# Low halves of the next batch's rotated query and key rows: from VectorE to GpSimd

## The chip, the core and the metric

One core of a Trainium2 chip runs the whole program. The metric is device time in microseconds (us). The engines are TensorE (PE: matrix products, with its weight loads as PEld), VectorE (DVE), ScalarE (ACT), GpSimd (POOL) and SyncE (SP, which here only issues DMAs). Each engine works off its own list of instructions in order, and waits on semaphores that the others raise.

## The reference

A post-norm decoder layer on x of 4 batches x 512 rows x 512 values: causal self-attention with 16 heads of 32 and keys and values from a latent of 128, then attention over 512 context rows that keeps the 54 highest scores, then a mixture of 8 experts, with a layer norm after each. The change touches the first block alone:

```
q = (x @ Wq).reshape(B, S, HEADS, HEAD_DIM).transpose(0, 2, 1, 3)
c_kv = x @ Wkv_down
k = (c_kv @ Wk_up).reshape(...)
v = (c_kv @ Wv_up).reshape(...)
q_rope = _apply_rope(q_rope, cos, sin)   # 24 of each head's 32 values; the same for k
scores = jnp.einsum('bhqd,bhkd->bhqk', qf, kf) * scale
weights = jax.nn.softmax(jnp.where(causal, -jnp.inf, scores), axis=-1)
out = jnp.einsum('bhqk,bhkd->bhqd', weights, v)
x = _layernorm(x + out)
```

## The kernel before

A product is made from 16-bit halves: each operand is split into a high half (rounded to f16) and a low half (what the rounding left), and three products high x high, high x low, low x high are summed. Queries and keys carry this in their transposed rows: `cat` holds, for each of the 8 row blocks of a batch (4 blocks of 128 rows, query and key of each), the high half twice and the low half once.

The first block works a batch at a time, and while it finishes the heads of batch b it already prepares batch b+1. Five lists, one for each computing engine (`A_PE`, `A_ACT`, `A_DVE`, `A_POOL`; SP's stands in code), set the order of the units by hand. A unit is a name and a number. The ones in this text:

- `row.i` (PE, line 952, then ACT, line 1240): the i-th block of queries (even i) or keys (odd i) is computed, and copied to the buffer `rows`, which has four places, i mod 4.
- `rope.i` (POOL, line 777): four instructions rotate that block in place: two multiplications (`turn_a`, `turn_b`, line 785), a subtraction (788) and an addition (790).
- `rhi.i` (ACT, line 1258): the high half goes into `cat`. `rlo.i` (DVE, lines 1545 to 1548): the low half is the difference of `rows` and the high half.
- `q0.i`, `k0.i`, `q1.i`, `k1.i` (PE, line 968): transposes of `cat`, copied out by DVE (q, line 1555) and ACT (k). They wait for `cat_lo`, which each `rlo` raises.
- `bq.i` and `max.i`: head i's scores with queries on the partitions, and their row maxima (DVE, four reductions, line 1566). `mT.i`: the maxima of four heads are transposed (PE) and copied into `qcT` (DVE, line 1576).
- `bk.i`, `exp.i`, `hi.i`, `lo.i`, `pv.i`: scores with keys on the partitions, their exponential (ACT), its high half (ACT) and low half (12 of the 16 heads, six by DVE and six by POOL, the latter at line 795), and the product with the values.
- `v.i`, `comb.i`, `res.i`: values of the next batch; heads put together; batch b-1's residual sum with its moments.
- `ln.0` (ACT a square root, DVE lines 1602 to 1609): batch b-1's layer norm. On DVE it is five small instructions (lines 1524 to 1528), and then four that scale 128x512 values each (line 1609).

The loop over b runs three times (b = 0, 1, 2); the last batch's heads follow without a next part. The first of the three has no `res` and no `ln`. The start-up lists, which prepare batch 0, are others (`A_START_DVE` and so on). A PSUM bank is shared by units as `A_BANK` says: `row.7` and `mT.2` both use bank 7, so PE's `row.7` waits until DVE has copied `mT.2` out. `row.6` waits so for `v.2`.

Of the kernel before, what the change touches and what calls it, by code (L numbers as in the profile page):

```python
# [30 lines left out]
TT = S // P  # L31
# [33 lines left out]
A_NEXT = ("xT", "c", "row", "rope", "rhi", "rlo", "v", "q0", "k0", "bqn", "maxn", "mTn")  # L65
# [15 lines left out]
def steps(text):  # L81

    return [(k, int(i)) for k, i in (word.split(".") for word in text.split())]
# [14 lines left out]
""")  # L98
A_DVE = steps("""
    xT.0 xT.1 q1.0 max.5 xT.2 xT.3 q1.1 res.0 lo.0 q1.2 max.6 res.1 c.0 q1.3  # L100
    max.7 res.2 mT.1 rlo.0 max.8 rlo.1 v.0 max.9 rlo.2 res.3 max.10 v.1 lo.4 rlo.3 max.11 v.2
    ln.0 max.12 rlo.4 mT.2 max.13 lo.6 q0.0 rlo.5 max.14 q0.1 comb.0 q0.2 max.15
    lo.8 rlo.6 rlo.7 q0.3 mT.3 maxn.0 comb.1 lo.12 maxn.1 comb.2 maxn.2
    lo.14 maxn.3 v.3 mTn.0 maxn.4 comb.3
""")
A_POOL = steps("""
    rope.0 lo.1 rope.1 lo.2 rope.2 rope.3 rope.4 rope.5 lo.5 rope.6 rope.7 lo.9
    lo.10 lo.13 
""")

# [21 lines left out]
def next_part(seq, kinds):  # L132
    return [u for u in seq if u[0] in kinds]
# [139 lines left out]
def decoder(nc, a):  # L273
    ctx = ExitStack()

    def sem(name):
        return ctx.enter_context(nc.semaphore(name))

    def sb(stack, name, shape, dt=F32):
        return stack.enter_context(nc.sbuf_tensor(name, shape, dt))  # L280

    with ctx:
# [31 lines left out]
        rows = sb(sa, "rows", [P, 4, H, HD])  # L314
# [3 lines left out]
        cat = sb(sa, "cat", [P, 2 * TT, H, 3, HD], F16)  # L318
# [99 lines left out]
        cat_hi = sem("cat_hi")  # L418
        cat_lo = sem("cat_lo")
# [80 lines left out]
        def a_upto(b, u):  # L500

            return b * A_PER[A_KIND.get(u[0], u[0])] + (u[1] + 1 + FREE)
# [231 lines left out]
        def _(pool):  # L734
# [40 lines left out]
            def heads(seq, b, nxt):  # L775
                for k, i in seq:
                    if k == "rope":

                        n, t = nxt * (2 * TT) + i, i // 2
                        pool.wait_ge(a_drained["row"], a_upto(nxt, ("row", i)))  # L780
                        pool.wait_ge(roped, n * 4 + FREE)
                        pair = rows[:, i % 4, :, NOPE:HD].rearrange("p h (i two) -> p h i two", two=2)
                        for j, dst in ((0, turn_a), (1, turn_b)):
                            cs = cossin[:, j, t].unsqueeze(1).to_broadcast([P, H, ROPE // 2, 2])
                            nc.gpsimd.tensor_tensor(dst[:, :, :, :], pair, cs, ALU.mult).then_inc(roped, 1)  # L785
                        pool.wait_ge(roped, n * 4 + (2 + FREE))
                        half = NOPE + ROPE // 2
                        nc.gpsimd.tensor_tensor(rows[:, i % 4, :, NOPE:half], turn_a[:, :, :, 0], turn_a[:, :, :, 1],
                                                ALU.subtract).then_inc(roped, 1)
                        nc.gpsimd.tensor_tensor(rows[:, i % 4, :, half:HD], turn_b[:, :, :, 1], turn_b[:, :, :, 0],  # L790
                                                ALU.add).then_inc(roped, 1)
                    elif k == "lo":

                        pool.wait_ge(p_hi, b * len(HALVED) + (HALVED.index(i) + 1))
                        nc.gpsimd.tensor_tensor(plo[:, i % 2, :], pf[:, i % 2, :], phi[:, i % 2, :], ALU.subtract).then_inc(p_lo_pool, 1)  # L795

            heads(next_part(A_POOL, A_NEXT), None, 0)
            pool.wait_ge(roped, 2 * TT * 4 + FREE)
            with pool.Fori(0, B - 1) as b:
                heads(A_POOL, b, b + 1)  # L800
            heads(own_part(A_POOL, A_NEXT), B - 1, None)


# [1177 lines left out]
```

## Time and profile before

| | |
|---|---|
| median of 3 runs | 1636.16 us (1635.18 to 1636.54) |
| the profiled execution | 1635.91 us, its span 1634.1 us |
| PE busy | 1471.2 us, 90% of the span |
| DVE, ACT, POOL busy | 1186.5, 900.4, 767.7 us |
| the three passes of the loop | 99 to 375 us of the span, roughly |

Times in the trace are us from the span's start. An instruction's duration in the trace runs from where its engine took it up, so it holds the time in which the engine stood on it. What an engine waited for before an instruction stands in brackets. The chain of waits is followed back from the last instruction: at each step to what released it. Its piece "issue" is time in which the profile shows no cause.

### The profile page before, as it was taken

The page shows a single profiled execution, that of the slowest core. Times are in us where ns is not written, and L with a number is a line of the kernel's source. Part 1 is how long each engine was busy: PE and PEld are TensorE (multiplying, and loading weights), DVE is VectorE, ACT ScalarE, POOL GpSimd, SP SyncE. Part 2 cuts the span into 40 slices and gives each one's busy share as a digit, 9 for nine tenths or more (in the row PEclk, how much of TensorE's full clock was granted, in tenths as well). Part 3 has the DMA queues.
Part 4 walks back from the last instruction along what each step waited for, and adds up shares of the span by engine and source line. Part 5 has one row for each costly group of instructions (what it writes and reads, how often), then busy time and mean ns, then how long its engine had stood idle before and what let it go on. Part 6 is the DMA issues. An engine that isn't in the chain of part 4 may idle for free.

```text
span 1634.1 us, 27867 instructions
## 1 busy us (share of the span) xinstructions
PE 1471.2 (90%) x10404; PEld 902.3 (55%) x10404; DVE 1186.5 (73%) x2030; ACT 900.4 (55%) x1452; POOL 767.7 (47%) x693
## 2 busy tenths in 40 slices
PE   6898888988788898587999999999999999999984
PEld 3466666566544454243665666566656665666554
DVE  4767787968459999967776667666766676667657
ACT  4367575766544553555465556555655565556542
POOL 5355362712212314888474456445644564456422
PEclk9799988988599999788999999999999999999997
DMA  9500010002011110210010001000110011000002
GB/s 288 213 27 2 29 53 29 27 28 104 27 52 52 52 53 1 65 66 13 27 40 26 27 26 36 31 27 27 35 32 27 26 29 37 27 27 28 12 1 103
DMA packets 68173, 74.72 MB, mean 46 GB/s; under 512 B 9021, under 2 KB 46525, under 8 KB 67017
## 3 DMA queue, kind: packets, MB, share of 16 engines
q1 hardware_dynamic: 67464, 68.73, 13.0%
q10 hardware_dynamic: 576, 4.19, 0.7%
q8 instruction: 88, 1.44, 0.4%
q14 instruction: 45, 0.36, 0.1%
HBM read 49.66 MB, written 10.49 MB: 37 GB/s over the span
## 4 chain that ended last, share of the span: by engine, by line
PE 65%; DVE 13%; issue 8%; POOL 6%; ACT 4%; DVEq 0%; ACTq 0%; POOLq 0%
PE banks L1177 48%; PE banks L920 6%; PE banks L1029 2%; PE banks L1013 2%; DVE nmf L1566 2%; PE banks L974 2%; PE banks L991 1%; POOL xsum L824 1%; POOL xsum L821 1%; ACT pf L1271 1%; DVE top L1698 1%; DVE wk L1694 1%; PE banks L1015 1%; DVE attf L1705 1%; POOL xc L829 1%
## 5 line engine op out<-in xcount | busy, mean ns | idle before, releaser
L1177 PE MATMUL banks<-xc,w 128*128 128x512 f16 x2688 | 588.7, 381 | 15.8 <-ACT banks L1220 15.8
L1177 PEld LDWEIGHTS banks<-xc,w 128*128 128x128 f16 x2688 | 263.7, 98 | 335.4 <-ACT banks L1220 21.2
L1177 PE MATMUL banks<-wd,mid 128*128 128x256 f16 x2688 | 296.5, 273 | 4.7 <-ACT banks L1220 2.8
L1177 PEld LDWEIGHTS banks<-wd,mid 128*128 128x128 f16 x2688 | 262.8, 98 | 39.3 <-ACT banks L1220 3.1
L897 POOL TENSOR_TENSOR mid<-m,mid 128x512 f16<-128x512 f32 x64 | 75.0, 1172 | 315.0 <-ACT mid L1220 314.9
L1220 ACT ACTIVATE banks<-banks 128x512 f32<-128x512 f32 x192 | 108.3, 578 | 186.5 <-PE banks L1177 186.5
L897 POOL TENSOR_TENSOR mid<-msum,mid 128x512 f16<-128x512 f32 x128 | 185.8, 1470 | 1.3 <-ACT mid L1220 1.3
L1511 DVE SCALAR_TENSOR_TENSOR w<-stage,w 128x512 f16<-128x512 f32 (+1 forms) x56 | 62.2, 1150 | 104.4 <-ACT w L1220 104.4
L1220 ACT ACTIVATE mid<-msum 128x512 f16<-128x512 f32 x128 | 81.1, 634 | 85.4 <-DVE msum L1881 29.2
L795 POOL TENSOR_TENSOR plo<-pf,phi 128x1280 f16<-128x1280 f32 x24 | 63.8, 2665 | 117.1 <-ACT phi L1220 116.9
L1566 DVE TENSOR_REDUCE nmf<-banks 128x1 f32<-128x512 f32 (+3 forms) x256 | 107.2, 481 | 10.2 <-PE banks L993 9.8
L1271 ACT ACTIVATE pf<-banks 128x1280 f32<-128x1280 f32 x64 | 79.1, 1236 | 38.9 <-PE banks L1015 21.9
L785 POOL TENSOR_TENSOR turn_a<-rows,cossin 128x384 f32<-128x384 f32 x32 | 35.9, 1123 | 121.1 <-ACT rows L1220 120.3
L1220 ACT ACTIVATE xc<-banks 128x512 f32<-128x512 f32 (+1 forms) x112 | 62.8, 598 | 49.5 <-PE banks L1124 28.5
L897 POOL TENSOR_TENSOR mid<-xc,mid 128x512 f16<-128x512 f32 x32 | 52.4, 1638 | 69.2 <-ACT mid L1220 69.2
L1013 PE MATMUL banks<-qcT,kcT 100*128 100x512 f16 (+3 forms) x256 | 71.4, 355 | 13.2 <-ACT pf L1271 11.8
L1511 DVE SCALAR_TENSOR_TENSOR wd<-stage,wd 128x512 f16<-128x512 f32 (+1 forms) x32 | 29.4, 960 | 65.9 <-ACT wd L1220 65.9
L1843 DVE TENSOR_TENSOR xc<-banks,xc 128x512 f32<-128x512 f32 x96 | 63.1, 683 | 17.3 <-ACT banks L1220 17.3
L1843 DVE TENSOR_TENSOR s<-banks,s 128x512 f32<-128x512 f32 x96 | 64.2, 684 | 14.1 <-PE banks L1177 14.0
L991 PE MATMUL banks<-kcT,qcT 96*128 96x512 f16 (+3 forms) x256 | 67.6, 338 | 5.2 <-DVE nmf L1566 3.9
L1220 ACT ACTIVATE s<-banks 128x512 f32<-128x512 f32 x96 | 56.3, 602 | 25.9 <-PE banks L1177 25.8
L1220 ACT ACTIVATE phi<-pf 128x1280 f16<-128x1280 f32 x48 | 60.9, 1269 | 1.2 <-PE banks L1034 1.2
(253 smaller groups left out, 2967.0 us busy)
## 6 DMA issues: line engine op xcount, KB each, us to landing
stage<-w_fold SPq DMA_DIRECT2D x24, 256.0 KB, 2.9
stage<-in_Wg SPq DMA_DIRECT2D x24, 256.0 KB, 3.2
stage<-in_Wu SPq DMA_DIRECT2D x24, 256.0 KB, 3.1
stage<-in_Wd SPq DMA_DIRECT2D x24, 256.0 KB, 2.8
vcat<-vnext SPq DMA_DIRECT2D x8, 528.0 KB, 3.3
x_in<-in_x SPq DMA_DIRECT2D x4, 1024.0 KB, 6.5
x_res<-in_x SPq DMA_DIRECT2D x4, 1024.0 KB, 5.8
c_raw<-in_ctx SPq DMA_DIRECT2D x4, 1024.0 KB, 5.5
```

The lines of the kernel that those rows point to most:

```text
L785: nc.gpsimd.tensor_tensor(dst[:, :, :, :], pair, cs, ALU.mult).then_inc(roped, 1)
L795: nc.gpsimd.tensor_tensor(plo[:, i % 2, :], pf[:, i % 2, :], phi[:, i % 2, :], ALU.subtract).then_inc(p_lo_pool, 1)
L897: nc.gpsimd.tensor_tensor(mid16[:, v % 3, 1, blk], mid_value(name), mid16[:, v % 3, 0, blk], ALU.subtract)\
L920: mm = nc.tensor.matmul(out, l(x, i), r(y, i), start=(i == 0 and j == 0), stop=(i == n - 1 and j == 2))
L991: nc.tensor.matmul(score[:, o:o + w], qcT[0:K3, i, t * P:(t + 1) * P], kcT[0:K3, i, 0:w], start=True, stop=False)
L1013: nc.tensor.matmul(st_ps[:, o:o + w], kcT[0:K3 + G, i, t * P:(t + 1) * P], qcT[0:K3 + G, i, t * P:S], start=True, stop=False)
L1177: mm = nc.tensor.matmul(out, l(x, i), r(y, i), start=start and i == 0 and j == 0, stop=stop and i == k - 1 and j == 2, skip_group_check=True)
L1220: return nc.scalar.activation(out, in_, ACT.Copy, scale=scale)
L1271: nc.scalar.activation(pf[:, i % 2, :], st_ps[:, 0:TRI], ACT.Exp, scale=1.0 / (SQ * SQ * math.sqrt(HD))).then_inc(exp_done, 1)
L1511: return stt(out=out, in0=src, scalar=scale, in1=hi, op0=ALU.mult, op1=ALU.subtract)
L1566: nc.vector.tensor_reduce(nmf[:, t, i % G:i % G + 1], max_bank(b, i)[:, o:o + w], AX, ALU.max, negate=True)\
L1843: tt_(saved, banks[:, k, :], saved, ALU.add).then_inc(c_sum, 1)
```

## The change

Eight units `rlo.0` to `rlo.7` leave DVE's list and go into POOL's. `rlo.i` stands there one rotation behind `rope.i`: `rlo.0` behind `rope.1`, and so on, with `rlo.7` last of them. `rlo.0` stands ahead of `lo.2`, `rlo.4` ahead of `lo.5`, and `rlo.7` ahead of `lo.9`. POOL gets the code for it, the same subtraction with the same wait for `rhi` (semaphore `cat_hi`), raising `cat_lo`. The start-up's `rlo` stay on DVE, so the call that prepares batch 0 now takes `rope` alone. No DMA, buffer or bank changes.

```
@@ -98,13 +98,13 @@
 A_DVE = steps("""
...
-    max.7 res.2 mT.1 rlo.0 max.8 rlo.1 v.0 max.9 rlo.2 res.3 max.10 v.1 lo.4 rlo.3 max.11 v.2
-    ln.0 max.12 rlo.4 mT.2 max.13 lo.6 q0.0 rlo.5 max.14 q0.1 comb.0 q0.2 max.15
-    lo.8 rlo.6 rlo.7 q0.3 mT.3 maxn.0 comb.1 lo.12 maxn.1 comb.2 maxn.2
+    max.7 res.2 mT.1 max.8 v.0 max.9 res.3 max.10 v.1 lo.4 max.11 v.2
+    ln.0 max.12 mT.2 max.13 lo.6 q0.0 max.14 q0.1 comb.0 q0.2 max.15
+    lo.8 q0.3 mT.3 maxn.0 comb.1 lo.12 maxn.1 comb.2 maxn.2
...
 A_POOL = steps("""
-    rope.0 lo.1 rope.1 lo.2 rope.2 rope.3 rope.4 rope.5 lo.5 rope.6 rope.7 lo.9
+    rope.0 lo.1 rope.1 rlo.0 lo.2 rope.2 rlo.1 rope.3 rlo.2 rope.4 rlo.3 rope.5 rlo.4 lo.5 rope.6 rlo.5 rope.7 rlo.6 rlo.7 lo.9
     lo.10 lo.13 
@@ -789,12 +789,16 @@
+                    elif k == "rlo":
+                        pool.wait_ge(cat_hi, nxt * (2 * TT) + (i + 1))
+                        dst = cat[:, i, :, 2] if i % 2 == 0 else cat[:, i, :, 1]
+                        nc.gpsimd.tensor_tensor(dst, rows[:, i % 4], cat[:, i, :, 0], ALU.subtract).then_inc(cat_lo, 1)
...
-            heads(next_part(A_POOL, A_NEXT), None, 0)
+            heads(next_part(A_POOL, ("rope",)), None, 0)
```

POOL's list inside the loop, before, from `rope.5` to `lo.5` (line 785 are the two multiplications of a rotation, 788 and 790 its end, 795 the low half of a head's exponentials):

```order
L780 REGISTER_ALU
L781 ISA
L785 TENSOR_TENSOR turn_a<-rows,cossin 128x384
L785 TENSOR_TENSOR turn_b<-rows,cossin 128x384
L786 REGISTER_ALU
L788 TENSOR_TENSOR rows<-turn_a 128x16x12
L790 TENSOR_TENSOR rows<-turn_b 128x16x12
L794 REGISTER_ALU
L795 TENSOR_TENSOR plo<-pf,phi 128x1280
```

The same place in the changed kernel, from `rlo.3` on; lines behind the new code have moved by four, so `lo` is line 799 and line 795 is the new subtraction:

```order
L795 TENSOR_TENSOR cat<-rows,cat 128x16x32
L780 REGISTER_ALU
L781 ISA
L785 TENSOR_TENSOR turn_a<-rows,cossin 128x384
L785 TENSOR_TENSOR turn_b<-rows,cossin 128x384
L786 REGISTER_ALU
L788 TENSOR_TENSOR rows<-turn_a 128x16x12
L790 TENSOR_TENSOR rows<-turn_b 128x16x12
L795 TENSOR_TENSOR cat<-rows,cat 128x16x32
L798 REGISTER_ALU
L799 TENSOR_TENSOR plo<-pf,phi 128x1280
```

Two `rlo` now stand around this rotation, and the second of them ahead of `lo.5`.

DVE's list in the loop, before, from the end of `ln.0` over `max.12` and `rlo.4` (line 1548) to `mT.2` (line 1576):

```order
L1609 TENSOR_SCALAR resid<-resid,mv,rstd 128x512 x4
L1564 ISA
L1566 TENSOR_REDUCE nmf<-banks 128x1
L1564 REGISTER_ALU
L1566 TENSOR_REDUCE nmf<-banks 128x1 x2
L1564 REGISTER_ALU
L1566 TENSOR_REDUCE nmf<-banks 128x1
L1546 REGISTER_ALU
L1548 TENSOR_TENSOR cat<-rows,cat 128x16x32
L1574 REGISTER_ALU
L1576 COPY qcT<-banks 4x2048
```

The same place in the changed kernel:

```order
L1613 TENSOR_SCALAR resid<-resid,mv,rstd 128x512 x4
L1568 ISA
L1570 TENSOR_REDUCE nmf<-banks 128x1
L1568 REGISTER_ALU
L1570 TENSOR_REDUCE nmf<-banks 128x1 x2
L1568 REGISTER_ALU
L1570 TENSOR_REDUCE nmf<-banks 128x1
L1578 REGISTER_ALU
L1580 COPY qcT<-banks 4x2048
```

`mT.2` now follows `max.12` directly.

## Rows read from the trace of the kernel before

**Rows 1.** The page, part 1: busy time, share, instructions of each engine.
```profile
PE 1471.2 (90%) x10404; PEld 902.3 (55%) x10404; DVE 1186.5 (73%) x2030; ACT 900.4 (55%) x1452; POOL 767.7 (47%) x693
```

**Rows 2.** Busy time, second pass: length, PE, PEld, DVE, ACT, POOL, PE clock, DMA.
```profile
188.00:281.00 93.00, 82.95 (x943) 59.94 (x942) 72.84 (x133) 64.91 (x85) 43.37 (x38) 0.89 0.11 36
```

**Rows 3.** Chain of waits, second pass: start, us, what it ran through.
```profile
199.12 0.71 POOL plo L795
...
208.38 0.92 POOL rows L790
...
222.12 1.14 issue
...
224.54 1.46 PE banks L920 x3
```

**Rows 4.** PE in time order at `row.7`: start, us, instruction, wait before it.
```profile
224.54 1.03 PE L920 MATMUL banks<-wku,cT 128*128 128x512 f16 x2 [2.35 <-DVE qcT L1576]
```

**Rows 5.** Busy time by stretch behind that wait, second and third pass (columns as Rows 2).
```profile
224.00:228.00 4.00, 3.46 (x20) 2.13 (x21) 3.57 (x6) 0.98 (x2) 3.17 (x5) 0.57 0.00 0
...
317.00:323.00 6.00, 5.71 (x33) 3.88 (x34) 5.09 (x9) 2.78 (x3) 5.09 (x6) 0.50 0.00 0
```

**Rows 6.** Line 1548, all of it: duration ns min/median/max, first and last start.
```profile
L1548 DVE TENSOR_TENSOR cat<-rows,cat x32: 674/693/1580, 28.0 to 332.5; 128x512 f16<-128x512 f32 x32
```

**Rows 7.** Line 808, a POOL subtraction of the same size and types in another stage.
```profile
L808 POOL TENSOR_TENSOR kq<-copyf,kq x16: 1152/1156/1161, 453.8 to 633.5; 128x512 f16<-128x512 f32 x16
```

**Rows 8.** POOL in time order, second pass.
```profile
201.66 1.44 POOL L785 TENSOR_TENSOR turn_a<-rows,cossin 128x384 f32<-128x384 f32 x1
...
215.24 0.99 POOL L785 TENSOR_TENSOR turn_a<-rows,cossin 128x384 f32<-128x384 f32 x1 [2.87 <-ACT rows L1220]
...
217.72 0.50 POOL L790 TENSOR_TENSOR rows<-turn_b 128x192 f32<-128x192 f32 x1
219.79 2.88 POOL L795 TENSOR_TENSOR plo<-pf,phi 128x1280 f16<-128x1280 f32 x1 [1.57 <-ACT phi L1220]
```

**Rows 9.** DVE in time order, second pass, ahead of it ACT's `v.1`.
```profile
210.29 0.64 ACT L1220 ACTIVATE vnext<-banks 128x128 f32<-128x128 f32 x2
...
212.12 1.59 DVE L1580 TENSOR_TENSOR plo<-pf,phi 128x1280 f16<-128x1280 f32 x1
213.63 0.68 DVE L1548 TENSOR_TENSOR cat<-rows,cat 128x512 f16<-128x512 f32 x1
...
216.64 0.16 DVE L1524 RECIPROCAL rstd<-rstd 128x4 f32<-128x4 f32 x1
...
220.11 1.68 DVE L1566 TENSOR_REDUCE nmf<-banks 128x1 f32<-128x512 f32 x4
221.70 1.52 DVE L1548 TENSOR_TENSOR cat<-rows,cat 128x512 f16<-128x512 f32 x1
223.26 1.23 DVE L1576 COPY qcT<-banks 4x2048 f16<-4x2048 f16 x1
```

**Rows 10.** POOL, then ACT, in time order, first pass.
```profile
125.53 0.99 POOL L785 TENSOR_TENSOR turn_a<-rows,cossin 128x384 f32<-128x384 f32 x1 [2.07 <-ACT rows L1220]
...
134.14 1.75 POOL L790 TENSOR_TENSOR rows<-turn_b 128x192 f32<-128x192 f32 x1
...
135.92 1.06 ACT L1220 ACTIVATE cat<-rows 128x1024 f16<-128x1024 f32 x1 [0.44 <-POOL rows L790]
```

**Rows 11.** Line 1609, all of it: duration ns min/median/max.
```profile
L1609 DVE TENSOR_SCALAR resid<-resid,mv,rstd x16: 539/544/547, 218.3 to 450.5; - x8, 128x512 f32<-128x512 f32 x8
```

**Rows 12.** DVE and POOL, a layer norm in the next stage, twice: POOL idle, POOL busy.
```profile
524.70 1.91 DVE L1742 TENSOR_SCALAR x2row<-x2row,mv,rstd 128x512 f32<-128x512 f32 x4
...
639.48 1.04 DVE L1525 TENSOR_TENSOR nwt<-rstd 128x4 f32<-128x4 f32 x1
...
642.10 3.71 DVE L1742 TENSOR_SCALAR x2row<-x2row,mv,rstd 128x512 f32<-128x512 f32 x4
643.27 1.33 POOL L824 TENSOR_TENSOR xsum<-xsum 128x512 f32<-128x512 f32 x1
```

## The prediction

> **What bounds the kernel now.** I read the page's busy times first, then the busy time by stretch over the loop's passes, then the chain of waits inside one pass, then each engine's list in time order where that chain changes engines. PE is busy for 90% of the span [rows 1], but in the second pass it is idle for some 10 of 93 us and its clock averages 0.89 of full speed [rows 2]; what a pass can gain or lose lies there. From 199 us on, the chain of waits runs through POOL (`lo.2`, `rope.2`, `rope.3`), through ACT's `v.1`, then through DVE (`lo.4`, `rlo.3`, `max.11`, `ln.0`, `max.12`, `rlo.4`, `mT.2`), and only then back to PE's `row.7` [rows 3]. The two engines between which the work moves thus stand one behind the other on that chain, and the question is which gains more.
>
> At `row.7` PE has stood for 2.35 us because `mT.2`'s bank was not copied out [rows 4], and after that its granted clock is at half, 1.2 GHz: 0.57 over 4 us in the second pass, 0.50 over 6 us in the third [rows 5]. Behind `row.7` PE works nearly without a gap, so a shift there moves the pass's end. The third pass repeats the second 92.8 us later. The first has no `ln.0`.
>
> **What leaves DVE.** Eight subtractions a pass. Alone one takes 0.69 us, but up to 1.58 [rows 6]: `rlo.0` stood behind POOL's `lo.2`, and POOL's next multiplication then stood behind it, 1.44 us instead of 0.99 [rows 8]. `rlo.4` took 1.52, right in front of `mT.2` [rows 9]. Were nothing else to change, `mT.2` would be copied out 1.5 us earlier. The `rlo` behind `mT.2` end no wait that PE feels, so I count them at nothing; DVE's idle time covers them.
>
> **What POOL gets.** Eight subtractions of 512 values. The trace has no such instruction on POOL for `cat`; the same size and types in another stage take 1.16 us, 1.15 to 1.16 in all 16 [rows 7]. The strided output might cost more; the multiplications, strided too, take 0.99 for 384 values [rows 8], which by count of values would be 1.32. I take 1.16, with 1.32 as the upper end; nothing in the trace is cheaper. Five of the eight stand ahead of `lo.5`. POOL now has waits to fill: 2.87 us for `row.5` and 1.57 for `hi.5` in the second pass [rows 8], 2.07 in the first [rows 10].
>
> **The second pass, POOL.** A rotation takes 2.98 us undisturbed (215.24 to 218.22) [rows 8]. From `lo.2`'s place at 199.1 [rows 3]: `rlo.0` to 200.2, `lo.2` (2.6) to 202.8, `rope.2` to 205.8, `rlo.1` to 207.5 (0.6 of that behind DVE's `res.3`, which now comes there), `rope.3` to 210.4. Now `rope.3` ends at 209.3 [rows 3], so it is 1.1 late. Then `rlo.2` to 211.6 and `rope.4`, with 1.4 us in which DVE's `lo.4` holds it, to 215.8; `rlo.3` to 216.9; `rope.5` would end at 219.8 alone, now 218.2. POOL has no wait left.
>
> **The second pass, DVE.** ACT does `rhi.3` before `v.1`, and `rhi.3` waits for `rope.3`. `v.1` ends on ACT at 210.9 now [rows 9], so 1.2 later, at about 212.1, then; DVE's own half of `v.1` follows it, and `lo.4` is issued at 212.7 rather than 212.12 [rows 9], stands behind a multiplication of `rope.4` until 213.5 and ends at 214.9. From there to `ln.0` takes 2.3 us (213.63 + 0.68 to 216.64) [rows 9]: `ln.0` starts at 217.2, against 216.64. All that DVE saved up to there has gone into waiting for ACT's `v.1`.
>
> Now comes the step that decides. `ln.0` takes 3.5 us today (216.64 to 220.11) [rows 9] since POOL is idle from 218.2 to 219.8 [rows 8]; the four scaling instructions never took over 0.55 [rows 11]. In the changed kernel POOL is busy throughout. What that does shows a stage later, where DVE does the same layer norm twice: with POOL idle its four scaling instructions take 1.91 us, and 3.71 beside POOL's subtractions of 1.3 us, one of which gets in between the first two; a small instruction ahead of them takes 1.04 [rows 12], where the one at 216.64 takes 0.16 [rows 9]. So the engines take turns: whoever waits goes next. POOL's turn in `ln.0` would hold the rest of `rope.5` (219.8 - 217.2 = 2.6), `rlo.4` (1.16), `lo.5` (2.6, ready because `hi.5` ends at 219.8 or a little later) and the next multiplication (1.0): 7.4 us, and DVE's own four 1.8. `ln.0` ends at 217.2 + 9.2 = 226.4, `max.12` (1.6) at 228.0, `mT.2` (1.23) at 229.2. Now `mT.2` ends at 224.5. The pass gets 4.7 us longer, although `rlo.4` is gone from in front of `mT.2`.
>
> From both sides: if `lo.5` and the multiplication fall behind the last scaling instruction, `ln.0` ends at 217.2 + 2.6 + 1.16 + 1.8 = 222.8, `mT.2` at 225.6, 1.1 late. If each of the eight instructions of `ln.0` that read SBUF with two inputs or scale waits out one POOL instruction (0.6, 1.0, 0.5, 0.5, 1.16, 2.6, 1.0, 1.0 = 8.4, and 2.6 of its own), it ends at 228.2, and `mT.2` 6.5 late. I take 4.7, near the upper end, because POOL's list has no gap there.
>
> On the scaling instructions a page of the Trainium skill speaks too. By its rows in this stage [rows 11] line 1609 has never paid for POOL. "SBUF — State Buffer", section "Who interferes with whom", says that VectorE instructions with two SBUF inputs, and `tensor_scalar` in a two-port mode, exclude GpSimd's, and that the one that comes second is blocked for the whole of the other. By that row alone `ln.0` would stay at 3.5 us, and the time would be that of the rival on the faster side below; by the rule it is the 4.7 us above. The trace agrees with the rule [rows 12].
>
> **The first pass.** No `ln.0`, but `rhi.6` on ACT waits for POOL's `rope.6` already, for 0.44 us [rows 10], and `k0.0`, `q0.1` and PE follow. Ahead of `rope.6` POOL gets five `rlo`, 5.6 us at a spacing of 1.12. It gives back the wait of 2.07 [rows 10] and some 2 us of holding: now it loses about 4.4 us there to instructions of DVE (134.14's 1.75 instead of 0.50 is one) [rows 10], later only two `lo` of 1.4. That leaves 1.6 us late, between 1.2 and 2.0.
>
> **The sum.** 1.6 + 4.7 + 4.7 = 11.0 us on the profiled execution's 1635.9: 1646.9. That execution lies 0.25 us under the median of the runs shown. PE's half clock I leave as it is: it stands 2.35 us today and gets the low clock, it will stand for 4 to 7 us and get it again; a longer stay at half could add 1.5 us a pass. The start-up and the last batch issue the same instructions as before, and SP's list is untouched.
>
> **Rivals.**
> - *`lo.5` falls behind the layer norm.* 1.6 + 2 x 1.1: 1639.7. For it: DVE slips through small gaps between POOL's instructions. Against it: four of them would have to go.
> - *Faster: DVE is the bound and POOL does not touch `ln.0`.* `mT.2` is copied 1.5 us earlier in two passes, PE stands 0.85 us instead of 2.35 and keeps its clock, which saves 0.43 x 4 = 1.7 and 0.5 x 6 = 3.0: -1.5 - 1.7 - 1.5 - 3.0 + 1.6 = -6.1, 1629.8. For it: line 1609 as it stands [rows 11]. Against it: the busy case [rows 12]. It decides from the point where the fourth scaling instruction ends before `lo.5` starts and `ln.0` starts no later than 216.7.
> - *Nothing measurable:* both hidden, 1635.9. Against it: both engines are on the chain [rows 3].
> - *All eight pay, and the half clock lasts longer:* 1.6 + 2 x (6.5 + 1.5) = 17.6, 1653.5.
>
> **How the numbers follow.** Forecast 1646.9 with its own range of 1643 to 1651: 0.61. All eight pay: 0.05. `lo.5` behind: 0.16. Nothing: 0.05. Faster: 0.13. The range 1637.5 to 1653.5 leaves out the faster case, nothing, and a little on top, 0.2. Within 0.2% (3.3 us, about what can be told from no change): the case of nothing, 0.05; slower 0.82, faster 0.13.
>
> **What would show it.** Right: no `cat` on DVE in the loop; POOL without a wait between `rope.1` and `lo.5`; `rope.3` about 1 us later, counted from `lo.2`'s old place; line 1613 (1609 before) over 2 us in one instance of a pass; `ln.0` 8 to 10 us long; PE's wait before `row.7` and inside `bq.13` together 6 to 7 us; the first pass 1 to 2 us longer. Wrong: scaling instructions of 0.54 throughout, or `lo.5` behind them; `row.7` without a wait and no half clock behind it; the `cat` subtraction on POOL far from 1.16.

## The result, and the profile after

The changed kernel takes 1642.4 us (median of 6 runs, 1640.1 to 1644.1) against 1635.1 (6 runs, 1630.8 to 1636.5): 7.3 us slower, ratio 1.0048 with a 95% interval of 1.0035 to 1.0062. The forecast was 11.0 us slower. All medians are of runs in the fast state; one run of pool_sub below, 2189.74 us at a mean clock of 0.64, was in the slow one and is left out. In the profiled execution, 1640.07 us, the busy times answer to [rows 1]: DVE lost 10.6 us, POOL gained 23.0. In the changed kernel's code the lines behind the new branch are four higher: 1613 is 1609 of before, 1580 is 1576, 924 is 920.

```profile
PE 1466.8 (90%) x10404; PEld 899.0 (55%) x10404; DVE 1175.9 (72%) x2006; ACT 900.2 (55%) x1452; POOL 790.7 (48%) x717
```

First the busy time by pass. A pass is cut where POOL starts `rope.0`; the third ends here where `lo.13` starts, since there is no next `rope.0` behind it. Columns as in [rows 2]: length, then busy time of PE, PEld, DVE, ACT, POOL, then PE's clock. Before:

```profile
99.17:188.40 89.23, 79.78 (x943) 58.53 (x941) 64.16 (x115) 61.61 (x81) 43.44 (x38) 0.92 0.04 14
188.40:281.16 92.76, 82.71 (x942) 59.78 (x940) 72.60 (x133) 64.69 (x84) 43.37 (x38) 0.89 0.11 36
281.16:347.85 66.69, 58.57 (x704) 41.66 (x701) 54.53 (x100) 49.83 (x65) 40.09 (x37) 0.94 0.05 17
sum 248.68, PE 221.07 PEld 159.97 DVE 191.29 ACT 176.12 POOL 126.90; mean PE 73.69 PEld 53.33 DVE 63.76 ACT 58.71 POOL 42.30
```

After:

```profile
98.75:190.52 91.77, 79.96 (x943) 58.59 (x942) 57.34 (x107) 61.43 (x81) 50.36 (x46) 0.93 0.04 14
190.52:286.10 95.58, 80.02 (x943) 57.61 (x941) 70.99 (x125) 64.46 (x84) 51.19 (x47) 0.93 0.10 35
286.10:355.09 68.99, 57.85 (x711) 40.80 (x709) 52.67 (x92) 49.74 (x65) 48.57 (x45) 0.95 0.05 17
sum 256.34, PE 217.84 PEld 157.00 DVE 181.01 ACT 175.63 POOL 150.13; mean PE 72.61 PEld 52.33 DVE 60.34 ACT 58.54 POOL 50.04
```

The passes are 2.5, 2.8 and 2.3 us longer, 7.7 in all, close to the loss of the medians. The two profiled executions as wholes are only 4.2 us apart (spans of 1634.1 and 1638.2 us): in the changed kernel the passes begin 0.4 us earlier, and from the third pass's `lo.13` to the end it takes 3.1 us less, for which I have no cause. PE's idle time (length less busy time) rose from 27.6 to 38.5 us, by 10.9. But PE's busy time fell by 3.2, as it ran at the full clock more of the time. "Lost to the half clock" below is PE's busy time by (1 - granted clock), summed over slices of 1 us: 18.1 us before, 13.9 after.

The second pass in detail. The chain of waits, where [rows 3] had POOL, `mT.2`, `row.7`:

```profile
202.31 2.61 POOL plo L799
...
211.89 0.52 POOL rows L790
...
221.86 1.24 DVE resid L1613
...
223.24 2.68 issue
225.92 1.21 DVE resid L1613
227.12 1.46 DVE nmf L1570 x4
...
230.03 1.47 PE banks L924 x3
```

Between `ln.0`'s scaling instructions stand 2.68 us without a shown cause. DVE's and then POOL's list in time order, answering to [rows 9] and [rows 8], show what lies there:

```profile
214.54 2.22 DVE L1584 TENSOR_TENSOR plo<-pf,phi 128x1280 f16<-128x1280 f32 x1
...
219.12 0.16 DVE L1528 RECIPROCAL rstd<-rstd 128x4 f32<-128x4 f32 x1
...
221.25 5.87 DVE L1613 TENSOR_SCALAR resid<-resid,mv,rstd  x4
227.04 1.67 DVE L1570 TENSOR_REDUCE nmf<-banks 128x1 f32<-128x512 f32 x4
228.75 1.23 DVE L1580 COPY qcT<-banks 4x2048 f16<-4x2048 f16 x1
```

```profile
207.84 1.60 POOL L795 TENSOR_TENSOR cat<-rows,cat 128x512 f16<-128x512 f32 x1
...
221.62 1.34 POOL L795 TENSOR_TENSOR cat<-rows,cat 128x512 f16<-128x512 f32 x1
222.92 2.79 POOL L799 TENSOR_TENSOR plo<-pf,phi 128x1280 f16<-128x1280 f32 x1
225.68 1.16 POOL L785 TENSOR_TENSOR turn_a<-rows,cossin 128x384 f32<-128x384 f32 x1
```

The four scaling instructions take 5.87 us; `rlo.4`, `lo.5` and the next multiplication fill that time on POOL. `ln.0` as a whole runs from 219.12 to 227.04, 7.9 us against 3.5. `mT.2`'s copy starts 38.23 us after the pass's start, 34.85 before. PE pays in two places instead of one [rows 4]: `bq.13` stands for `max.12`, then `row.7` for `mT.2`. Its list, second pass:

```profile
227.78 0.61 PE L995 MATMUL banks<-kcT,qcT 96*128 96x512 f16 x1 [4.01 <-DVE nmf L1570]
...
230.03 1.46 PE L924 MATMUL banks<-wku,cT 128*128 128x512 f16 x3 [0.45 <-DVE qcT L1580]
```

In the first pass `rhi.6` on ACT now waits 1.91 us for `rope.6`, where [rows 10] had 0.44, and ends 1.4 later, counted from the pass's start:

```profile
136.94 1.06 ACT L1224 ACTIVATE cat<-rows 128x1024 f16<-128x1024 f32 x1 [1.91 <-POOL rows L790]
```

PE feels it in front of `q0.1`, a wait that the kernel before did not have there (`osb` is ACT's copy of finished products with the values):

```profile
139.12 0.65 PE L978 MATMUL banks<-ident,cat 128*96 128x128 f16 x8 [1.67 <-ACT osb L1224]
```

### The profile page after: what moved, and what is told of

It reads as the page before. It is cut to its first block, busy times and chain, and to the rows that moved or that the text cites. A ratio compares the mean times of both kernels' runs of the same rounds, so it can differ in the third digit from the quotient of the medians.

```text
span 1638.2 us, 27854 instructions
## 1 busy us (share of the span) xinstructions
PE 1466.8 (90%) x10404; PEld 899.0 (55%) x10404; DVE 1175.9 (72%) x2006; ACT 900.2 (55%) x1452; POOL 790.7 (48%) x717
## 4 chain that ended last, share of the span: by engine, by line
PE 62%; DVE 12%; issue 11%; POOL 8%; ACT 4%; DVEq 0%; POOLq 0%; ACTq 0%
PE banks L1181 48%; PE banks L924 5%; PE banks L1033 2%; POOL plo L799 1%; PE banks L978 1%; DVE nmf L1570 1%; PE banks L1017 1%; PE banks L995 1%; DVE top L1702 1%; DVE wk L1698 1%; POOL turn_b L785 1%; DVE attf L1709 1%; PE banks L1128 1%; POOL mid L901 1%; POOL xsum L828 1%
## 5 line engine op out<-in xcount | busy, mean ns | idle before, releaser
L1017 PE MATMUL banks<-qcT,kcT 100*128 100x512 f16 (+3 forms) x256 | 68.0, 342 | 12.9 <-ACT pf L1275 11.8
```

Of the source, the lines that this page charges most:

```text
L1017: nc.tensor.matmul(st_ps[:, o:o + w], kcT[0:K3 + G, i, t * P:(t + 1) * P], qcT[0:K3 + G, i, t * P:S], start=True, stop=False)
```

## The experiments

My theory was that POOL's load delays `ln.0` in passes 2 and 3 and the rotations in the first. The rivals: VectorE's relief is worthless, the later low halves cost the time, or any load on POOL does. Two measures separate them. One is when the copy of `mT.2` starts, counted from the pass's start: in each kernel it agrees to 0.04 us between both passes and, where a kernel was profiled twice, between the executions. The other is PE's idle time over the three passes. "Four" is the time of `ln.0`'s four scaling instructions, second pass. Each ratio is against the kernel before on the same chip; it is not the quotient of the two medians and can differ from it by some 0.1%. The kernel before has a median in each of four sets of runs. The second profiles were single executions of 1638.2 us (before) and 1643.1 us (after).

| kernel | time, us | ratio (95%) | `mT.2` | four | idle | lost to half clock |
|---|---|---|---|---|---|---|
| before, two profiles | 1633.5 to 1635.1 | | 34.85 | 1.92 | 27.6, 26.7 | 18.1, 17.4 |
| after, two profiles | 1642.4 | 1.0048 (1.0035 to 1.0062) | 38.23 | 5.87 | 38.5, 37.8 | 13.9, 13.7 |
| no_sub | 1624.0 | 0.9953 (0.9936 to 0.9969) | 32.37 | 2.06 | 28.4 | 6.9 |
| pool_sub | 1654.5 | 1.0141 (1.0118 to 1.0163) | 41.62 | 6.37 | 40.8 | 22.1 |
| after_ln_gap | 1634.1 | 1.0000 (0.9986 to 1.0014) | 32.65 | 1.92 | 33.0 | 13.0 |
| before_ln_gap | 1638.0 | 1.0028 (1.0015 to 1.0041) | 32.26 | 6.51 | 34.4 | 17.0 |
| lo5_late | 1643.6 | 1.0066 (1.0048 to 1.0084) | 36.60 | 4.26 | 34.1 | 19.6 |
| after_both | 1640.4 | 1.0043 (1.0026 to 1.0060) | 32.65 | 1.91 | 36.4 | 20.8 |
| split | 1629.9 | 0.9972 (0.9962 to 0.9983) | 32.25 | 4.21 | 26.2 | 19.5 |
| rlo_behind | 1635.3 | 1.0012 (0.9997 to 1.0026) | 33.41 | 1.91 | 34.2 | 13.6 |
| split_ln | 1634.2 | 1.0000 (0.9987 to 1.0013) | 33.42 | 1.92 | 30.0 | 10.1 |
| split_end | 1632.7 | 0.9993 (0.9979 to 1.0007) | 32.26 | 1.91 | 27.3 | 16.5 |

**Relief without load (no_sub).**

```diff
-  nc.gpsimd.tensor_tensor(dst, rows[:, i % 4], cat[:, i, :, 0], ALU.subtract).then_inc(cat_lo, 1)
+  pool.sem_inc(cat_lo, 1)
```

> The changed kernel, but GpSimd only waits and signals where it should subtract: the low halves of batches 1 to 3 are not made at all. So VectorE is relieved and GpSimd gets no work. Theory (what GpSimd's eight subtractions hold up is the whole loss): ln.0 about 3.5 us in passes 2 and 3, mT.2 about 1.5 to 2.2 us earlier than before in each, row.7 nearly without a wait, first pass no longer than before; 1627 to 1632 us against 1635 before. Rival (relieving VectorE is worth nothing, the passes are set by GpSimd's rotations and ScalarE): 1634 to 1636.

9.5 us faster than before, 3 us beyond my range. So the relief is worth something; that rival falls. (`cat_lo` is also raised at once here, so VectorE's relief and the earlier signal are not told apart.) DVE's list in the second pass, which starts at 184.16:

```profile
212.84 2.06 DVE L1613 TENSOR_SCALAR resid<-resid,mv,rstd  x4
214.83 1.67 DVE L1570 TENSOR_REDUCE nmf<-banks 128x1 f32<-128x512 f32 x4
216.53 1.23 DVE L1580 COPY qcT<-banks 4x2048 f16<-4x2048 f16 x1
```

The step from one to the other is not what I thought, though. `mT.2` is 2.5 us early, yet PE's idle time is as before (28.4); the gain lies in the half clock, 6.9 us against 18.

**Load without relief (pool_sub).**

```diff
-    rope.0 lo.1 rope.1 lo.2 rope.2 rope.3 rope.4 rope.5 lo.5 rope.6 rope.7 lo.9
+    rope.0 lo.1 rope.1 sub.0 lo.2 rope.2 sub.1 rope.3 sub.2 rope.4 sub.3 rope.5 sub.4 lo.5 rope.6 sub.5 rope.7 sub.6 sub.7 lo.9
...
+  elif k == "sub":
+      pool.wait_ge(cat_hi, nxt * (2 * TT) + (i + 1))
...
+      nc.gpsimd.tensor_tensor(spare[:, i % 2], wku[:, 0]..., wku[:, 1]..., ALU.subtract).then_inc(spared, 1)
```

> The kernel before, with all its subtractions left on VectorE, and eight more subtractions of the same size a pass on GpSimd, at the places of the change, whose results nobody reads. So the load without the relief and without any new dependence between the engines. Theory (GpSimd's load holds up VectorE's ln.0 and the rotations): at least the whole loss of the change, +7, and up to +11 since rlo.4 still stands ahead of mT.2: 1642 to 1647 us. Rival (the loss comes from the low halves being ready later, not from the load): 1635 to 1637.

21.0 us slower. No other unit waits for what these subtractions make, so the load by itself costs, and the rival of later low halves is not needed. The load is dearer than I gave it: `mT.2` is 6.8 us late. Load and relief do not add up (21.0 - 9.5 = 11.5, measured 7.3): with both, DVE's own subtractions are no longer in POOL's way, which I take for the reason but did not try.

**`ln.0` elsewhere (after_ln_gap, before_ln_gap).** The same move in both kernels:

```diff
-    ln.0 max.12 mT.2 max.13 lo.6 q0.0 max.14 q0.1 comb.0 q0.2 max.15
-    lo.8 q0.3 mT.3
+    max.12 mT.2 max.13 lo.6 q0.0 max.14 q0.1 comb.0 q0.2 max.15
+    lo.8 ln.0 q0.3 mT.3
```

> The changed kernel with VectorE's ln.0 moved from ahead of max.12 to ahead of q0.3, where VectorE waits for TensorE anyway. Theory (the loss of passes 2 and 3 is ln.0 taking turns with GpSimd): it goes, max.12 starts about 219 as counted in the second pass before, mT.2 is copied out 2 us earlier than before; only the first pass's 1.5 to 2.5 us stay: 1630 to 1635 us. Rival (GpSimd's load or the late rope.3, rhi.3, v.1 is the cost, wherever ln.0 stands): 6 to 8 us above the same move made in the kernel before.

> The kernel before with the same move of ln.0 to ahead of q0.3, behind rlo.7. Theory: ln.0's 3.5 us leave the chain ahead of mT.2, row.7 loses its wait of 2.35 us in two passes, q0.3 comes up to 0.8 us later: 1629 to 1632 us, and under 4 us below the changed kernel with the same move (the first pass's loss and a late v.1). Rival (ln.0 is not on the chain that sets the passes): 1634 to 1637.

The changed kernel gets all its loss back with this move alone. Not all of that is the meeting with POOL: the move also takes `ln.0` off the chain ahead of `mT.2`, and by split against split_ln below that is worth 4.3 us even where `ln.0` had met nothing (1.92 us in split_ln). And 5.4 us of idle time more than in the kernel before are still there, most of it in front of `q0.1` (1.7 in each pass). So how much of the 7.3 us the meeting makes is not isolated. In the moved place `ln.0` finds POOL idle: DVE's list, then POOL's, second pass:

```profile
223.74 1.23 DVE L1580 COPY qcT<-banks 4x2048 f16<-4x2048 f16 x1 [2.37 <-PE banks L1005]
...
241.81 1.92 DVE L1613 TENSOR_SCALAR resid<-resid,mv,rstd  x4
```

```profile
243.59 5.19 POOL L799 TENSOR_TENSOR plo<-pf,phi 128x1280 f16<-128x1280 f32 x2 [4.33 <-ACT phi L1224]
```

The kernel before loses 4.5 us by it, which I had not expected. `rlo.6` and `rlo.7` still stand ahead of `ln.0` there, and `lo.9` and `lo.10` come while it scales. DVE, POOL and PE in its second pass:

```profile
242.07 6.51 DVE L1609 TENSOR_SCALAR resid<-resid,mv,rstd  x4
```

```profile
242.64 5.65 POOL L795 TENSOR_TENSOR plo<-pf,phi 128x1280 f16<-128x1280 f32 x2 [9.09 <-ACT phi L1220]
```

```profile
249.23 0.61 PE L1001 MATMUL banks<-ident,nm 128*128 128x128 f16 x4 [3.89 <-DVE qcT L1555]
```

The same four instructions cost 1.92 or 6.51 us, by what POOL does in that moment, and PE pays 3.89 us for it at once. A miss of mine, and the cleanest evidence for the mechanism: no `rlo` on POOL is needed for it.

**`lo.5` later (lo5_late, after_both).** after_both has the move of `ln.0` as well.

```diff
-    ... rope.5 rlo.4 lo.5 rope.6 rlo.5 rope.7 ...
+    ... rope.5 rlo.4 rope.6 rlo.5 lo.5 rope.7 ...
```

> The changed kernel with GpSimd's lo.5 (2.6 us) moved behind rope.6 and rlo.5. Theory (GpSimd's longest instruction falls between the scaling instructions of ln.0, and rope.6 is late): the gap that lo.5 fills takes a multiplication of 1.0 us instead, ln.0 about 1.6 us shorter in passes 2 and 3, and rope.6, rhi.6 about 2.6 us earlier in each pass: 4 to 6 us below the changed kernel, so 1634 to 1638 us at 1633.5 before. Rival (any load on GpSimd costs the same, whatever its order): 1640 to 1643. Third: pv.5 waits for the later lo.5 and the pass gains nothing.

> The changed kernel with ln.0 moved to ahead of q0.3 and lo.5 moved behind rope.6 and rlo.5. The first move alone gave 1634.1 against 1633.5 before, with ln.0's scaling instructions at 1.92 us just ahead of lo.9. Theory: the late rope.6 and rhi.6 (TensorE then waits 3.0 us for osb in that kernel's second pass) go too, 1.5 to 2.5 us a pass: 1627 to 1631 us. Rival: osb is late for another reason, 1633 to 1635.

In lo5_late the four scaling instructions shrink from 5.87 to 4.26, the 1.6 us expected, and the wait at the first pass's `q0.1` is gone. But in the first pass the third case came true: PE waits for the late `lo.5`. In the other two passes of lo5_late it doesn't; in after_both it does in each pass, for 3.1 us, and its 1640.4 us lie above both cases of its expectation. PE's list, first pass of lo5_late, then second pass of after_both:

```profile
138.15 0.21 PE L1036 MATMUL banks<-vcat,phi 128*128 128x33 f16 x1 [3.12 <-POOL plo L799]
...
234.31 0.19 PE L1036 MATMUL banks<-vcat,phi 128*128 128x33 f16 x1 [3.07 <-POOL plo L799]
```

In lo5_late PE's idle time falls by 4 us against after, what it loses to the half clock rises by 6, and the time stays.

**Only the last three on POOL (split), and what does it (split_ln, split_end, rlo_behind).** split, against the kernel before:

```diff
-    ln.0 max.12 rlo.4 mT.2 max.13 lo.6 q0.0 rlo.5 max.14 q0.1 comb.0 q0.2 max.15
-    lo.8 rlo.6 rlo.7 q0.3 mT.3 ...
+    max.12 mT.2 rlo.4 max.13 lo.6 q0.0 max.14 q0.1 comb.0 q0.2 max.15
+    lo.8 ln.0 q0.3 mT.3 ...
-    ... rope.5 lo.5 rope.6 rope.7 lo.9
+    ... rope.5 lo.5 rope.6 rlo.5 rope.7 rlo.6 rlo.7 lo.9
```

POOL's `rlo` here also waits for the `rlo` before it (on `cat_lo`), since two engines now raise that semaphore. split_ln puts `ln.0` back ahead of `max.12`; split_end puts it behind `comb.3`, last in the pass. rlo_behind is the kernel before with `mT.2 rlo.3 max.13 lo.6 q0.0 rlo.4` instead of `rlo.3` ahead of `max.11` and `rlo.4` ahead of `mT.2`.

> Only rlo.5, rlo.6 and rlo.7 on GpSimd, behind rope.6 and rope.7, where it has most gaps; rlo.0 to rlo.4 stay on VectorE, rlo.4 behind mT.2; ln.0 ahead of q0.3. Theory: GpSimd is not later than before up to rope.6, so the first pass loses nothing, and ln.0 finds GpSimd idle: 1626 to 1631 us. Rival (ln.0 again meets lo.9, as it did where VectorE kept all eight, 6.51 us for four scaling instructions): 1635 to 1639.

> The kernel before with rlo.3 and rlo.4 moved behind mT.2 and q0.0 on VectorE; no work on GpSimd added. It prices the relief ahead of mT.2 by itself. Theory: mT.2 about 2 us earlier in each pass, row.7 waits 0.3 us instead of 2.35, and of the half clock behind it some goes: 1628 to 1631 us. Rival (VectorE's relief is worth nothing; what rlo.3 and rlo.4 free, others need as late): 1633 to 1636.

> The split kernel (rlo.5 to rlo.7 on GpSimd, rlo.4 behind mT.2) with ln.0 back ahead of max.12. Tells what its 4.6 us come from. If from GpSimd's part (VectorE relieved late in the pass) : 1629 to 1632 us, as GpSimd is idle at ln.0 (3.5 us). If from moving ln.0 off the chain: back at 1633 to 1636.

> The split kernel with ln.0 at the end of VectorE's pass, behind comb.3, where GpSimd stands idle for 20 us and VectorE waits 2.9 us for ScalarE's xT.0. In split its four scaling instructions took 4.21 us since lo.9 came between; here 1.9. Theory (turns with GpSimd are what ln.0 costs): 1626 to 1630 us, up to 3 us below split. Rival: xT.0 comes 0.7 us late at the head of the next pass, which eats it: 1629 to 1633.

split beats both kernels: 4.6 us below before, 12.5 below after by medians from different chips. Its `ln.0` still meets `lo.9` (238.09 on DVE, 4.21 us), which its theory did not expect, but DVE waits for PE just there: for 2.71 us in the kernel before, whose `rlo.6` and `rlo.7` took another 1.28. split_ln only equals before, so the gain hangs on moving `ln.0` off the chain, the second case of its expectation. split_end removes the meeting (1.91 us) and is not faster than split; its idle time and passes agree with split's to about 1 us, and why its median is 2.8 us higher I can't tell from one profile of each. rlo_behind and split_ln both have `mT.2` 1.4 us early without a gain: PE waits elsewhere then, in rlo_behind 1.4 us for a later query transpose.

**The two kernels again (before_2, after_2).**

> The kernel before, unchanged, profiled a second time. In the first profile TensorE stood idle for 27.5 us of the three passes (99.17 us to the last lo.13) and lost 18.1 us of its busy time to the half clock (busy time by (1 - granted clock), in pieces of 1 us). If waits set the idle time, it comes back within 1 us; the clock's part may differ by one or two stretches of 3.4 us each. Rival (the idle time is as much by chance as the clock): off by more than 3 us.

> The changed kernel, unchanged, profiled a second time. First profile: 38.5 us idle in the three passes, 11.0 more than before, and 13.9 us lost to the half clock, 4.2 less than before. If the clock pays part of the change back for a reason, the loss is again below that of before; if by chance, it is 13 to 22 us, anywhere around before's. Idle time within 1 us of 38.5.

The sums over the same three stretches, before_2 and then after_2:

```profile
sum 247.07, PE 220.35 PEld 159.97 DVE 191.53 ACT 176.31 POOL 127.01; mean PE 73.45 PEld 53.33 DVE 63.84 ACT 58.77 POOL 42.34
```

```profile
sum 255.87, PE 218.04 PEld 156.54 DVE 181.23 ACT 175.57 POOL 150.24; mean PE 72.68 PEld 52.18 DVE 60.41 ACT 58.52 POOL 50.08
```

Idle time is 26.7 and 37.8 us, within 0.9 of the first pair; the half clock again takes less in the changed kernel, 13.7 us against 17.4. PE's busy time falls by 2.3 us here and 3.2 in the first pair, so two or three of the 11 us come back; two pairs are few. Over both pairs the passes are 8.2 us longer. As wholes, these two executions are 4.9 us apart.

## Why the prediction was right, and where its sizes were off

- *What POOL's subtraction costs.* Forecast 1.16 us, measured 1.15 in the middle; 1.60 where DVE's `res.3` was in the way, as counted for `rlo.1`:

```profile
L795 POOL TENSOR_TENSOR cat<-rows,cat x24: 1147/1155/1607, 109.0 to 337.3; 128x512 f16<-128x512 f32 x24
```

- *DVE's saving is eaten by the wait for `v.1`.* Right. `rope.3` ends 1.0 us later within its pass (forecast 1.1), `ln.0` starts 0.4 later (forecast 0.6), POOL has no wait from `rope.1` to `rope.6`.
- *`ln.0` takes turns with POOL.* The mechanism is right, and shown by after_ln_gap and before_ln_gap. The prediction drew on the Trainium skill, "SBUF — State Buffer", section "Who interferes with whom": the instruction that comes second is blocked for the whole of the other. The 5.87 and 6.51 us agree. Of the other direction, POOL behind a scaling instruction, the rows show 0.17 to 0.19 us (next point), less than that instruction's own 0.54. Line 1609's earlier record of never over 0.55 [rows 11] only meant that POOL had been idle.
- *4.7 us a pass.* Here the size was off: `mT.2` is 3.4 us late, `ln.0` 7.9 us long and not 8 to 10, and PE's waits at `bq.13` and `row.7` come to 4.5 us and not 6 to 7. The failed step is "7.4 us, and DVE's own four 1.8". POOL's part was 7.7 us (219.12 to the end of the multiplication, 226.84), but of DVE's 1.8 us only some 0.2 came on top. The rest runs beside POOL's next instruction: `rlo.4`, `lo.5` and the multiplication are only 0.17 to 0.19 us longer than undisturbed (1.34 against 1.15, 2.79 against 2.62, 1.16 against 0.99).
- *The first pass.* Forecast 1.6, measured 2.5 and 2.2 in the two pairs. But after_ln_gap, whose first pass issues the same instructions, takes 89.25 us for it, against 89.23 in the kernel before; the half clock took 3.4 us there and 6.3 in after:

```profile
101.84:191.09 89.25, 77.45 (x943) 56.70 (x942) 58.03 (x107) 61.42 (x81) 50.38 (x46) 0.96 0.04 14
```

So the pass's length does not test this term. The step to `q0.1` is right: it comes 1.4 us later in all three.
- *"PE's half clock I leave as it is."* Wrong: over the passes PE lost 4.2 and 3.7 us less to it in the two pairs. The stretch around `row.7` is there in both, 0.57 over 8 us in the changed kernel where [rows 5] had 0.57 over 4. A second stretch in the second pass of the kernel before is missing in the changed one. Before:

```profile
238.00:246.00 8.00, 7.30 (x99) 5.95 (x100) 2.99 (x5) 7.50 (x10) 5.14 (x2) 0.58 0.01 2
```

After, the stretch around `row.7` and the part of the pass that answers to the row above:

```profile
226.00:234.00 8.00, 5.77 (x34) 3.18 (x35) 7.40 (x12) 1.55 (x3) 5.75 (x7) 0.57 0.00 0
...
242.00:250.00 8.00, 5.31 (x93) 4.44 (x93) 3.64 (x5) 7.19 (x9) 4.52 (x3) 1.00 0.01 2
```

In the row of before PE ran mostly at 1.2 GHz and was busy for 7.30 of 8 us; in the second row of after it runs at 2.4 GHz and is busy for 5.31, waiting for ACT in between (0.93, 1.35 and 0.41 us). But this need not come from the change: the kernel before has the same in its own third pass, as far from the pass's start as the first row is in the second. The busy time, then PE's longest wait in it:

```profile
330.76:338.76 8.00, 5.31 (x106) 4.44 (x106) 4.23 (x5) 7.60 (x9) 4.05 (x2) 1.00 0.01 2
```

```profile
335.98 0.65 PE L974 MATMUL banks<-ident,cat 128*96 128x128 f16 x8 [1.35 <-ACT osb L1220]
```

So idle time and half clock partly replace each other already between two passes of one kernel. In the second and third passes of its two profiles, the kernel before had the second stretch twice and lacked it twice; the changed kernel lacked it all four times. That the longer wait at `bq.13` is the reason is not shown, and what decides in which pass the clock falls was not settled.
- *The sum.* 11.0 us of time was forecast from three terms; PE's idle time rose by 10.9 and 11.1. The agreement is partly luck, as the terms came out at 2.4, 5.5, 3.0 and 3.9, 3.1, 4.1 in the two pairs instead of 1.6, 4.7, 4.7, with waits among them that I had not named. The time rose by 7.3.

## What to carry to other kernels

Before moving work to GpSimd, look not only at its idle time but at what VectorE does beside the new instructions: one short chain of scaling instructions on the critical path cost 4 us more once GpSimd had no gap there. Put such a VectorE unit where GpSimd is idle or VectorE waits anyway: its placement was worth 8 us in the changed kernel, as much as the whole loss, and some 4 of that lay in leaving the critical path. On TensorE count idle time and time lost to the half clock apart, since one can take the other's place from pass to pass.

## What was not expected of the hardware

- The blocking was uneven. A scaling instruction of 0.54 us on VectorE waited for whole instructions of GpSimd (four took 5.87 and 6.51 us), while in after it lengthened GpSimd's by only 0.17 to 0.19 us each.
- The time of one point inside a pass repeated to 0.04 us (`mT.2` at 34.84 to 34.86 in four passes of two executions), while whole runs of the same kernel spread over 1629 to 1639 us. In the first pass of after, its second profile and after_ln_gap, which issue the same instructions, PE's idle time is 11.8, 12.5 and 11.8 us, and the loss to the half clock 6.3, 4.5 and 3.4.
